# Turning batch-norm coefficients on TensorE instead of through DRAM, in a two-layer convolution kernel

## The reference, cut to what matters

```python
x = x + _L0_conv_ref(_gn(x), weight, bias)          # 64 -> 64 per channel
u = _gn(x)                                          # per image and group of 16 channels
m = mean(u, (0, 2, 3)); v = var(u, (0, 2, 3))       # batch norm 1: per channel, over all images
h = sign((u - m) * rsqrt(v + 1e-5) * g1 + be1)
h = conv3x3(h, sign(conv_w) * sw, groups=16)        # sw: one scale per output channel
h = batchnorm(h, g2, be2)                           # batch norm 2: again over all images
h = h + u
x = x + where(h > 0, h, prelu_a * h)
```

## Time and profile before

| | us |
|---|---|
| median of 3 runs | 4591.73 (4591.44 to 4593.64) |
| profiled execution | 4591.19 |
| its span | 4589.1 |
| busy: TensorE, VectorE, ScalarE, GpSimd | 4297.1, 4173.0, 3861.6, 1476.0 |

### The profile page before, as it was taken

One profiled execution on the slowest core, in us unless ns is written; L12 is line 12 of the kernel. 1 busy time (PEld: TensorE's weight loads), 2 busy tenths in 40 slices (PEclk: granted clock), 3 DMA queues, 4 the chain that ended last, 5 costly groups with the idle time before them and its releaser, 6 DMA issues.

```text
span 4589.1 us, 82259 instructions
## 1 busy us (share of the span) xinstructions
PE 4297.1 (94%) x21948; PEld 2702.5 (59%) x21948; DVE 4173.0 (91%) x9963; ACT 3861.6 (84%) x5517; POOL 1476.0 (32%) x3480
## 2 busy tenths in 40 slices
PE   6999999999999997999999995999999999999998
PEld 6999999999999994444444442444444444444443
DVE  6999999999999997999899987999999999999998
ACT  7999999999999995888888885777777777777776
POOL 3888888888888883000000000000000000000000
PEclk9999999999999998999999998999999999999999
DMA  5888888888888889999999997999999999999998
GB/s 198 317 318 320 316 316 323 314 319 322 316 317 318 320 302 315 385 385 385 385 385 385 385 385 289 383 389 388 389 387 386 390 387 389 387 388 387 388 387 308
DMA packets 686230, 1612.18 MB, mean 351 GB/s; under 512 B 30002, under 2 KB 423986, under 8 KB 620658
## 3 DMA queue, kind: packets, MB, share of 16 engines
q1 hardware_dynamic: 686194, 1611.76, 95.7%
HBM read 940.55 MB, written 671.10 MB: 351 GB/s over the span
## 4 chain that ended last, share of the span: by engine, by line
PE 51%; SPq 20%; ACT 11%; DVE 9%; issue 8%; DMA 1%; DVEq 0%; ACTq 0%; POOL 0%
PE psV L1019 17%; SPq L359 12%; PE psT L1002 10%; DVE ring_x L958 8%; SPq L383 7%; PE psT L1104 5%; PE psV L1016 5%; PE psT L1106 5%; PE psV L1106 4%; PE psV L1104 4%; ACT ring_y L678 3%; ACT ring_z L678 3%; ACT ring_g L584 2%; PE psV L1100 1%; ACT late L668 1%
## 5 line engine op out<-in xcount | busy, mean ns | idle before, releaser
L1019 PEld LDWEIGHTS psV<-W0T,ring_gT 128*128 128x128 f32 x8192 | 1077.0, 192 | 33.7
L1019 PE MATMUL psV<-W0T,ring_gT 128*128 128x128 f32 x8192 | 1080.2, 275 | 0.0
L773 DVE BATCH_NORM_STATS2 early<-ring_z 128x6 f32<-128x128 f32 x4096 | 822.6, 274 | 0.0
L764 DVE SCALAR_TENSOR_TENSOR ring_z<-psV,x_r,ring_x 128x1024 f32<-128x1024 f32 x512 | 657.3, 1284 | 117.6 <-DVE early L773 76.9
L668 ACT ACTIVATE late<-ring_x,minus_b 128x512 f32<-128x512 f32 x1024 | 639.6, 707 | 0.9 <-PE psV L1106 0.9
L848 DVE BATCH_NORM_STATS2 h_tup<-ring_x 128x6 f32<-128x512 uint16 x1024 | 630.7, 678 | 0.5
L632 ACT ACTIVATE ring_x<-ring_x,bn_c 128x1024 f16<-128x1024 f32 x512 | 604.1, 1230 | 31.0 <-DMA bn_c<-bn_scratch 31.0
L481 POOL TENSOR_SCALAR ring_y<-ring_z,u_r,u_nm 128x1024 f32<-128x1024 f32 x512 | 605.7, 1199 | 35.6 <-POOL gn L500 35.6
L590 ACT ACTIVATE ring_g<-ring_x,x_ms 128x1024 f32<-128x1024 f32 x512 | 585.2, 1143 | 0.0
L577 ACT ACTIVATE ring_gT<-psT 128x1024 f32<-128x1024 f32 x512 | 523.7, 1023 | 49.2 <-PE psT L1002 23.7
L678 ACT ACTIVATE ring_y<-ring_y,gnb 128x512 f32<-128x512 f32 x512 | 368.1, 801 | 211.2 <-DVE ring_x L958 175.7
(11 more groups left out here) (153 smaller groups left out, 5682.8 us busy)
## 6 DMA issues: line engine op xcount, KB each, us to landing
ring_x<-in_x SPq DMA_DIRECT2D x128, 2048.0 KB, 8.8
y_scratch<-ring_y SPq DMA_DIRECT2D x128, 2048.0 KB, 12.8
ring_x<-y_scratch SPq DMA_DIRECT2D x512, 512.0 KB, 7.6
out<-ring_x SPq DMA_DIRECT2D x256, 1024.0 KB, 14.4
h_scratch<-ring_x SPq DMA_DIRECT2D x256, 512.0 KB, 7.8
ring_y<-y_scratch SPq DMA_DIRECT2D x128, 1024.0 KB, 8.1
ring_z<-y_scratch SPq DMA_DIRECT2D x128, 1024.0 KB, 8.2
ring_g<-h_scratch SPq DMA_DIRECT2D x64, 1024.0 KB, 12.2
```

The source lines that it names most:

```text
L764: dve.scalar_tensor_tensor(out=ring_z[:, c % 2, cols], in0=psV[:, j % 2, :], scalar=x_r[:, s, j:j + 1], in1=ring_x[:, s, cols], op0=ALU.mu ...
L773: last = dve.bn_stats(z_tup[:, s, j, 2 * r:2 * r + 2, :].rearrange("p h t -> p (h t)"), ring_z[:, c % 2, SL * j + 2 * S * r:SL * j + 2 * S ...
L1019: last = pe.matmul(psV[:, j % 2, P * r:P * (r + 1)], ring_gT[:, j, P * r:P * (r + 1)], W0T[:, :], start=False, stop=(r % 4 == 3))
```

## The change

Four edits.

1. Batch norm 1: the mean and the variance, by group in PSUM, are each spread over a [32 x 128] tile with a 0/1 mask (`bn1_m`), and one small matmul with four mask columns gives them by channel in `psV`. The epsilon, the power and the coefficients are then taken by channel, and `bn1_c` is written by VectorE. `gb1` has the layout by channel for that. The store, the load and their semaphores are gone.
2. Batch norm 2: the coefficients by channel are spread by eight masked multiplications into `bn2_m`, and two matmuls with sixteen mask columns give them by group in `psT`, on all 128 partitions. VectorE reads `minus_b2`, `scale_l` and `bn2_q` from there. VectorE then waits itself for all h stores to have landed. One more constant is loaded, `route` (128 x 36, the masks).
3. The last unit of pass 1 is normalised by ScalarE, with a semaphore of its own (`y_last`), and no more by GpSimd.
4. SP's order around batch norm 2: each of the last three h stores goes ahead of one load of pass 3, and all four slots of pass 3 are loaded there, no more three.

```diff
-                             (gb1[:, 0, :], g1.rearrange("(q j) -> q j", j=GC)),
-                             (gb1[:, 1, :], be1.rearrange("(q j) -> q j", j=GC)),
+                             (pick[:, :], pick_in), (route[:, :], route_in),
+                             (gb1[:, 0, :], g1.rearrange("(k p) -> p k", p=P)),
+                             (gb1[:, 1, :], be1.rearrange("(k p) -> p k", p=P)),
@@ SP, after pass 1
-            store_y(loops1, SLOTS - 1)
-            sp.wait_ge(bn1_ready, 1)
-            sp.dma_start(bn1_dram..., bn1_q...).then_inc(bn1_out, 16)
-            sp.wait_ge(bn1_out, 16)
-            sp.dma_start(bn1_c[:, :, :], bn1_dram...).then_inc(bn1_in, 16)
+            sp.wait_ge(y_last, NQ)
+            sp.dma_start(y_unit[B - 1], ring_y[:, 1, :]).then_inc(y_stored[1], 16)
@@ SP, after pass 2
-            for c in range(3):
-                load_3(0, c)
             for c in range(1, SLOTS):
                 store_h(loops2, c)
+                load_3(0, c - 1)
+            load_3(0, SLOTS - 1)
             for s in range(SLOTS):
                 sp.wait_ge(h_stored[s], 16 * (T2 // SLOTS))
-            (wait bn2_ready, store bn2_c, wait bn2_out, four loads of bn2_q)
@@ SP, pass 3: the load moves under the same condition as the store
                 if from_round(i, c, 1):
                     sp.wait_ge(added, 8 * t)
-                if until(i, c, T3 - 3):
-                    load_3(i, c + 3)
-                if from_round(i, c, 1):
+                    if until(i, c, T3 - 3):
+                        load_3(i, c + 3)
                     store_out(i, c - 1)
@@ GpSimd
-            for j in range(NQ):
-                normalise_z(last, SLOTS - 1, j)
-            pool.wait_ge(bn1_step, 15)
-            pool.tensor_tensor(bt[0:GROUPS, 9, :], bt[0:GROUPS, 8, :], minus_half[0:GROUPS, :], ALU.pow)
+            pool.wait_ge(bn1_step, 17)
+            pool.tensor_tensor(bt[:, 9, 0:J], bt[:, 8, 0:J], minus_half[:, 0:J], ALU.pow)
@@ ScalarE, after pass 1
+            act.wait_ge(u_small, B)
+            act.wait_ge(y_stored[1], 16 * (B // 2 - 1))
+            for j in range(NQ):
+                act.activation(ring_y[:, 1, :]...[:, j], ring_z[:, 1, SL * j:SL * (j + 1)]...,
+                               ACT.Identity, bias=u_nm[:, SLOTS - 1, j:j + 1],
+                               scale=u_r[:, SLOTS - 1, j:j + 1]).then_inc(y_last, 1)
-            act.wait_ge(bn1_in, 16)
+            act.wait_ge(bn1_ready, 1)
@@ VectorE, batch norm 1
+            own = route[few, 0:8].unsqueeze(2).to_broadcast([GROUPS, 8, GC])
+            for n in range(2):
+                step(dve.tensor_tensor(bn1_m[:, n, :]..., psT[few, n, 0:GC]..., own, ALU.mult), bn1_step, done)
+                if n == 0:
+                    dve.wait_ge(bn1_var, 1)
+            dve.wait_ge(bn1_routed, 2)
+            step(dve.tensor_scalar(bt[:, 8, 0:J], psV[:, 1, 0:J], EPS, None, ALU.add), bn1_step, done)
             (gain times power, mean times that, offset minus that: as before, now [128, 4] into bn1_c)
@@ VectorE, batch norm 2
-            dve.wait_ge(bn2_in, 64)
-            (minus_b2 and scale_l from bn2_q)
+            own = route[:, 12:20].unsqueeze(1).to_broadcast([P, J, 8])
+            for n in range(2):
+                dve.wait_ge(bn2_ready, n + 1)
+                for m in range(4):
+                    last = dve.tensor_tensor(bn2_m[:, n, 32 * m:32 * m + 32]..., bn2_c[:, :, n]..., own, ALU.mult)
+                last.then_inc(bn2_masked, 1)
+            dve.wait_ge(bn2_routed, 2)
+            (minus_b2, scale_l and bn2_q from psT: three tensor_scalar)
+            dve.wait_ge(bn2_scaled, 3)
+            for s in range(SLOTS):
+                dve.wait_ge(h_stored[s], 16 * (T2 // SLOTS))
@@ TensorE
+            for n in range(2):
+                pe.wait_ge(bn1_step, 15 + n)
+                pe.matmul(psV[:, n, 0:J], bn1_m[:, n, :], route[0:GROUPS, 8:12]...).then_inc(bn1_routed, 1)
@@ TensorE, after pass 2
+            for n in range(2):
+                pe.wait_ge(bn2_masked, n + 1)
+                pe.matmul(psT[:, n, 0:GC], bn2_m[:, n, :], route[:, 20:36]...).then_inc(bn2_routed, 1)
```

More of the change, by code:

```diff
@@ L115, in two_layer_kernel @@
         minus_half = sb("minus_half", [P, GC])
-        gb1 = sb("gb1", [GROUPS, 2, GC])
+        gb1 = sb("gb1", [P, 2, J])
         gb2 = sb("gb2", [P, 2, J])
@@ L305, in row @@
                 "a p n f -> (a p) n f")
-        N_CONST = 15
+        N_CONST = 16
         SCALES = 8
@@ L824, in _ @@
             step(dve.tensor_tensor(bt[:, 10, :], bt[:, 7, :], bt[:, 5, :], ALU.add), bn1_step, done)
[L825 removed]
             few = slice(0, GROUPS)
[L827 removed]
+            own = route[few, 0:8].unsqueeze(2).to_broadcast([GROUPS, 8, GC])
+            for n in range(2):
+                step(dve.tensor_tensor(bn1_m[:, n, :].rearrange("p (a j) -> p a j", a=8),
+                                       psT[few, n, 0:GC].unsqueeze(1).to_broadcast([GROUPS, 8, GC]), own, ALU.mult),
+                     bn1_step, done)
+                if n == 0:
+                    dve.wait_ge(bn1_var, 1)
+            dve.wait_ge(bn1_routed, 2)
+            step(dve.tensor_scalar(bt[:, 8, 0:J], psV[:, 1, 0:J], EPS, None, ALU.add), bn1_step, done)
             dve.wait_ge(bn1_pow, 1)
[L829 to L831 removed]
+            step(dve.tensor_tensor(bn1_c[:, :, 0], gb1[:, 0, :], bt[:, 9, 0:J], ALU.mult), bn1_step, done)
+            step(dve.tensor_tensor(bt[:, 11, 0:J], psV[:, 0, 0:J], bn1_c[:, :, 0], ALU.mult), bn1_step, done)
+            dve.tensor_tensor(bn1_c[:, :, 1], gb1[:, 1, :], bt[:, 11, 0:J], ALU.subtract).then_inc(bn1_ready, 1)
             WIDE = SLOTS * BATCH
@@ L928, in _ @@
             step(dve.tensor_tensor(hb[:, 8, :, 1], gb2[:, 0, :], scale_w[:, :], ALU.mult), bn2_step, done)
-            step(dve.tensor_tensor(bn2_c[:, :, 0], hb[:, 8, :, 1], hb[:, 7, :, 0], ALU.mult), bn2_step, done)
+            dve.tensor_tensor(bn2_c[:, :, 0], hb[:, 8, :, 1], hb[:, 7, :, 0], ALU.mult).then_inc(bn2_ready, 1)
+            dve.wait_ge(bn2_ready, 1)
             step(dve.tensor_scalar(hb[:, 5, :, 0], hb[:, 5, :, 0], 0.5, None, ALU.mult), bn2_step, done)
@@ L1064, in _ @@
             pe.matmul(psT[:, 1, 0:GC], quarter[:, :], bt[:, 10, :], start=True, stop=True).then_inc(bn1_var, 1)
+            for n in range(2):
+                pe.wait_ge(bn1_step, 15 + n)
+                pe.matmul(psV[:, n, 0:J], bn1_m[:, n, :], route[0:GROUPS, 8:12], start=True, stop=True).then_inc(bn1_routed, 1)
             pe.wait_ge(bn1_ready, 1)
@@ L1089, in _ @@
             rounds(pe, pass2, T2, 2 * HEAD)
+            for n in range(2):
+                pe.wait_ge(bn2_masked, n + 1)
+                pe.matmul(psT[:, n, 0:GC], bn2_m[:, n, :], route[:, 20:36], start=True, stop=True).then_inc(bn2_routed, 1)
             pe.wait_ge(diag_done, 1)
@@ L1126, in constants @@
                 pick[row, 5 + n] = 1.0
+    route = np.zeros((P, 36), np.float32)
+    group, part = np.arange(GROUPS), np.arange(P)
+    route[group, group % 8] = 1.0
+    route[group, 8 + group // 8] = 1.0
+    route[part, 12 + part // GC] = 1.0
+    route[part, 20 + part % GC] = 1.0
     return {"identity": np.eye(P, dtype=np.float32), "quarter": quarter,
-            "algebra": np.ascontiguousarray(np.concatenate([sel, sel], axis=2)), "pick": pick}
+            "algebra": np.ascontiguousarray(np.concatenate([sel, sel], axis=2)), "pick": pick, "route": route}
 def kernel(**inputs):
```

48 lines of the change are left out of this document (19 added, 29 removed).

## The result

| | before | after | ratio, 95% interval |
|---|---|---|---|
| median of 6 runs each, us | 4591.66 (4591.44 to 4593.64) | 4574.91 (4573.96 to 4576.4) | 0.9963 (0.9952 to 0.9973) |
| profiled execution, us | 4591.19 | 4573.96 | |
| its span, us | 4589.1 | 4572.2 | |

The kernel is 16.75 us faster by the medians and 16.9 by the spans. The forecast was 18.6 and 4573. To see where the difference sits, both spans are cut at the same events. The last column is the difference.

A forecast was written before the change was run, and what follows sets the result against it. Passes 2 and 3 keep the transfer engines full, so only the two restarts and the start count: -6.9 - 12.5 + 0.8 = -18.6 us, 4572.6 profiled, 4573 for the median; the range of 8 in 10 is 4568 to 4579.5.

The forecast's parts named there:

- the first hand-over: From pass 1 to pass 2, at batch norm 1: the restart comes 6.9 us earlier, bounds 3.9 and 7.5.
- Quiet GpSimd, -2.8: End of pass 1: with ScalarE normalising the last unit, eight VectorE steps shorten from 4.74 to 1.9 us; bounds 0 and 2.9.
- Masks and matmuls +1.2, power -1.9, round trip -3.3, last steps -0.1: Batch norm 1: masks and matmuls add time; a 4-column power, no DRAM trip and 4-column last VectorE steps save it.
- Cover by the last y store, 0.4 to 1.2 us: Pass 2's restart: the last y store lands 0.4 to 1.2 us before sign 0 ends, so the sign releases SP's loads.
- Second hand-over, -12.5: From pass 2 to pass 3: VectorE begins pass 3 at 2822.0 in place of 2834.54; bounds 10.5 and 13.6.
- two arms nearly level: Second hand-over: coefficients ready at 2821.4, last conv words landed at 2821.7 to 2823.5; the later sets pass 3's start.
- Start, +0.8: Kernel start: one more constant and 960 more one-element descriptors cost 0.8 us; bounds 0.3 and 2.5.
- Pass 1 and pass 2 unchanged: Inside the passes: the change touches no work there; pass 2 stays as long as before within 2 us.
- the slower rival: Pass 3: another rhythm of loads and stores; 0.145 us more a step eats the 18.6, 0.2 gives 4598.6; chance 0.04.
- The signs that were named: Changed profile: pass 2's first load behind sign 0, pass 3 2.5 to 3 us after the coefficients, ScalarE at about 20.5.
- Of the other rivals, the first: Both restarts wait for a landing store: gains 3.9 at the first, 10 at the second, total -13, 4578; chance 0.18.
- the first gain isn't passed on: Pass 2: its last load depends on something the earlier restart doesn't move, so -6.9 becomes 0; 4584; chance 0.06.

The follow-up runs named there:

- e_undo3: The changed kernel with GpSimd normalising the last unit of pass 1 again, in place of ScalarE; 4578.66 us, ratio 0.9970.
- e_wait: The changed kernel with VectorE's wait for the last h stores moved behind pass 3's first combining instructions; 4573.55 us, ratio 0.9958.
- e_order: The changed kernel with SP's order at batch norm 2 as h store, load 0, the last two h stores, then loads 1 to 3; 4572.60 us, ratio 0.9957.
- e_undo4: The changed kernel with SP's old order at batch norm 2, three pass 3 loads ahead of the last three h stores; 4580.28 us, ratio 0.9973.
- e_double: The changed kernel with two more one-element loads of 512 elements each among the constants, into an unread tile; 4575.85 us, ratio 0.9965.
- e_route: The changed kernel with only the load of the masks (route) issued after unit 2's load; 4576.02 us, ratio 0.9963.
- e_only4: The kernel before with only SP's new order at batch norm 2, coefficients still through DRAM; 4600.82 us, ratio 1.0019.
- e_best2: The changed kernel with gb1, gb2, route loaded late, last two h stores before loads 1-3, VectorE's h-store wait later, slopes before unit 1's load; 4565.02 us, ratio 0.9941.
- e_only3: The kernel before with only the last unit's normalisation moved from GpSimd to ScalarE; 4589.81 us, ratio 0.9994 (0.9985 to 1.0004).
- e_late: The changed kernel with the loads of gb1, gb2 and route issued after unit 2's load; 4572.40 us, ratio 0.9957.

## Why the prediction was right

Measured 4574.91 against 4573, and -16.9 against -18.6 by the spans. Two terms were mis-sized by 1.2 us each, both to the same side, and the first hand-over came 0.3 better; no large errors cancelled. Step by step:

- *Quiet GpSimd, -2.8.* Right: e_undo3 puts it at 3.03, a little above the upper bound of 2.9, and 2.9 where the loads restart. ScalarE's four pieces took 4.63 for a forecast of 5.0 and lay beside other work, as the step said.
- *Masks and matmuls +1.2, power -1.9, round trip -3.3, last steps -0.1.* With the step above the sum was -6.9; the table has -7.2. The four instructions of the two small matmuls take 1.04, the power 1.03. These were not tried one by one, but as a block: e_undo3 has them and not the quiet GpSimd, and its first sign comes 4.17 us earlier after the last cell than before (14.79 less 10.62), for a forecast of 4.1. The trip of 3.3 us that went is measured in the kernel before. The 2 us for a transfer that the prediction quotes from the Trainium skill ("DMA: Bandwidth & Descriptors") stand there in a section on transfers that GpSimd issues; here SP issues them, and the sum rightly went by the rows.
- *Cover by the last y store, 0.4 to 1.2 us.* Gone, by 0.15 us. Counted from the last cell, the store went out at 2.3, earlier than the 2.8 of the step, but took 7.8 us to land (the profile's figure) where the step had 7.1: it landed at 10.1 in place of 9.9. The sign meanwhile ended at 10.0 in place of 10.3. Small errors on both sides used up the cover, which the step had as thin as 0.4 us. In this kernel and in the eight experiments that keep both ScalarE's normalisation and the mask layout, the load follows the store's issue by 7.86 to 7.98 us; in e_undo3 it follows the sign. That the loads restart -7.0 and the sign -7.2 is this.
- *Second hand-over, -12.5.* Measured -11.3, and this is one of the two terms that were off; the arm that was mis-sized is the landing of the last words. Counted from the last unpacked words, the coefficients came at 15.4 where the step had 15.7, so that arm was right. The words landed at 17.4 where it had 16.0. The step had the transfers run at 397 GB/s from 4.7 us ahead of the last unpack. The windows of the kernel after give 273 GB/s there (first row) and 396 only behind it:

```profile
2794.80:2800.30 5.50, 4.12 (x21) 1.68 (x18) 5.50 (x10) 2.32 (x3) 0.00 (x0) 1.00 0.83 273
2800.30:2817.70 17.40, 1.03 (x4) 0.93 (x4) 12.63 (x51) 0.00 (x0) 1.04 (x1) 0.62 1.02 396
```

  5.5 us at 124 GB/s less are 0.68 MB, which take 1.7 us at 396; by this estimate the slow stretch makes up the 1.4 us that the landing was late. The mechanism, two arms nearly level, was right; I had called them level within a microsecond, and they stand 2.1 apart. e_wait and e_order, which each take the landing out, give those 2.1 back.
- *Start, +0.8.* Measured +2.0 (+1.8 to +2.2 over e_undo3, e_undo4, e_wait and e_order), inside its bounds of 0.3 and 2.5 but the most undersized term. The step counted packets at the rate of a microsecond in which the engines had a full queue (1554 of them). In the kernel after the packets pass at that rate too (1571 of them from 11 to 12 us), but then the engines run short: SP, held at the loads in front, issues unit 1's load only at 12.83, and the last constants wait behind that load. The time idle from 12 to 16 us is, by the estimate above, 1.4 of the 2.0, and the step had no term for it. e_double and e_route show that the single prices don't add up to it (0.5 a load at the margin, nothing for the masks). How the 2.0 divide between the one-element loads and the order in which they fall is open.
- *Pass 1 and pass 2 unchanged.* The +1.0 and -1.2 of the table are not the change. The stretch to the last cell is 1726.4 to 1727.0 in before, e_undo3, e_undo4, e_only4, e_order, e_double and e_best2, and 1727.4 to 1727.8 in the others, e_only3 among them, which touches nothing ahead of it; and e_undo3 and e_undo4 have the very same program there as the kernel after. Pass 2 is 1043.3 twice and 1044.3 to 1045.2 otherwise. So these two differences are what one execution differs from the next by, and they nearly cancel. The last section shows where the first arises; why pass 2 takes 1.2 us less in two executions is open.
- *Pass 3.* 1753.8 to 1755.5 in all thirteen kernels. With 128 steps, the 0.145 us a step of the slower rival would be 18.6; it isn't there. Load 3 ahead of the first stores has no effect beyond this spread.
- *The signs that were named.* Two came otherwise. SP's first load of pass 2 was to follow sign 0 and follows the landing of a y store. And VectorE was to begin pass 3 at 2.5 to 3 us after the last coefficient step; it begins 4.0 after it (2817.81 less 2813.81), with the h store as its idle time's cause. ScalarE's first instruction was to come at about 20.5 and came at 21.68.

Of the other rivals, the first was right in kind: both restarts hang on a landing store now. Its price was wrong: it had the two restarts 3.0 and 2.5 us behind the forecast, and they came 0.1 ahead of it and 1.2 behind. So the time is nearer to the forecast's 4573 than to its 4578. That the first gain isn't passed on is refuted by pass 2, which is no longer than before. The prediction did not say how strongly edits 2 and 4 depend on each other; tried singly in the kernel before, the order is a loss.

## What to carry to other kernels

Where one queue carries all transfers, a tiny transfer costs what stands ahead of it, so take small round trips off the path before reordering the large ones, and price the two together. When two arms meet at a restart, count how each stands from a common event, and look at the rate in the stretch before it, not only in the one behind. Constants that are needed late belong behind the first loads of data, and constants that are needed first ahead of the second one: that was worth 8 us here, half as much as the whole change.

## What the runs showed of the hardware that was not expected

- A 4 KB store needed 1.35 us on a drained queue, 3.01 right behind the last words at the second place, and 16.07 with 6 MB ahead of it (e_only4).
- SP is held by its own issues when one-element loads are in line: 2.07 us at one of 512 elements in the kernel after, 4.05 in e_late. But the same kind of load holds it for 0.44 in e_best2, ahead of one with 3.62. A hold avoided at one issue turns up at the next (e_route), so these figures are no prices.
- TensorE's granted clock at the start of pass 1 differs between executions of the same work. The windows from 53 to 59 us of the kernel after, and of e_undo4 behind them (clock: third number from the end), with the same start and the same program there:

```profile
53.00:56.00 3.00, 1.20 (x6) 1.52 (x8) 0.00 (x0) 3.00 (x5) 0.00 (x0) 0.55 0.02 5
56.00:59.00 3.00, 3.00 (x15) 2.84 (x14) 0.12 (x1) 1.36 (x4) 1.41 (x3) 0.50 0.00 0
```

```profile
53.00:56.00 3.00, 1.55 (x7) 1.50 (x8) 0.00 (x0) 3.00 (x5) 0.00 (x0) 1.00 0.02 5
56.00:59.00 3.00, 3.00 (x22) 2.83 (x22) 0.81 (x1) 1.38 (x4) 1.39 (x3) 1.00 0.00 0
```

  From 56 to 59 one has 1.2 GHz and 15 matmuls, the other 2.4 GHz and 22. The second eviction to `ring_z` begins 1.4 us later after the start in the first (62.67 less 21.68) than in the second (61.28 less 21.71), which is the whole difference of the two stretches to the last cell (1.3). The same holds in all thirteen kernels: from the begin of that eviction to the last cell they take 1686.6 to 1686.9 us, so their spread of 1.4 us in that stretch lies ahead of it. The six with the longer stretch have 3.5 to 3.9 us from the first eviction's begin to the second's, the other seven 3.1.
